# The large mamba stage of a hybrid model: layer-norm turn, channels and step sizes in one block, and the causal convolution as four lagged matrix products

## The reference, cut to what matters

```python
D_MODEL = 128; D_INNER = 256; D_STATE = 16; D_CONV = 4; DT_RANK = 64
residual = x
h = _layernorm(x, ln_g, ln_b)
x_and_res = h @ W_in.T                       # 512 channels
x_h, res = jnp.split(x_and_res, [D_INNER], axis=-1)
xc = jnp.swapaxes(x_h, 1, 2)
xc = lax.conv_general_dilated(xc, conv_w, window_strides=(1,), padding=[(D_CONV - 1, 0)],
                              dimension_numbers=('NCH', 'OIH', 'NCH'), feature_group_count=D_INNER)
x_h = jax.nn.silu(jnp.swapaxes(xc + conv_b[None, :, None], 1, 2))
x_dbl = x_h @ W_x.T
dt, Bm, Cm = jnp.split(x_dbl, [DT_RANK, DT_RANK + D_STATE], axis=-1)
dt = jax.nn.softplus(dt @ W_dt.T + b_dt)
y = _selective_scan(x_h, dt, Bm, Cm, A) + x_h * D_param
y = y * jax.nn.silu(res)
out = y @ W_out.T
return residual + alpha * out
```

## Time and profile before

| | us |
|---|---|
| median of 3 runs | 3471.79 |
| the runs | 3464.45 to 3476.44 |
| the profiled execution | 3465.48 |
| its span in the trace | 3463.7 |

### The profile page before, as it was taken

How to read it: one execution, slowest core, us unless ns; L and a number is a source line. 1 busy time by engine, 2 the same in 40 slices (tenths; PEclk the granted TensorE clock), 3 DMA queues, 4 the chain that set the end, 5 groups by cost and what they waited for, 6 DMA issues and landing times. The chain is left out here.

```text
span 3463.7 us, 62367 instructions
## 1 busy us (share of the span) xinstructions
PE 2799.8 (81%) x21875; PEld 1638.3 (47%) x21951; DVE 2446.1 (71%) x4011; ACT 1755.5 (51%) x3569; POOL 1872.4 (54%) x1198
## 2 busy tenths in 40 slices
PE   3677478568999984999999994677677599999997
PEld 1211266443344431777577751223222277757774
DVE  5599746558777762777577755798699677767764
ACT  3544124134565653777377732543444277637762
POOL 3499211131222212988198812797299598729871
PEclk9699678779999996999999996899799899999999
DMA  3365000033232211122112200343154121212121
GB/s 90 79 164 152 8 1 6 8 114 70 44 51 42 49 22 34 37 44 43 27 41 43 44 21 6 122 158 110 46 167 158 45 44 41 45 25 44 41 45 40
DMA packets 177166, 205.29 MB, mean 59 GB/s; under 512 B 108854, under 2 KB 122893, under 8 KB 176397
## 3 DMA queue, kind: packets, MB, share of 16 engines
q1 hardware_dynamic: 176876, 201.51, 22.9%
HBM read 138.36 MB, written 9.44 MB: 43 GB/s over the span
## 5 line engine op out<-in xcount | busy, mean ns | idle before, releaser
L319 POOL TENSOR_TENSOR arena<-arena 128x1024 f32<-128x1024 f32 x192 | 451.3, 2351 | 61.2 <-DVE arena L336 34.3
L1462 DVE TENSOR_REDUCE causal_peak_parts<-psum 128x1 f32<-128x512 f32 (+3 forms) x608 | 374.9, 657 | 123.0 <-PE psum L1320 79.6
L2060 POOL TENSOR_TENSOR arena<-arena,w_minus_half 128x16 f32<-128x16 f32 x128 | 372.7, 2912 | 95.0 <-DVE arena L1967 95.0
L1429 ACT ACTIVATE arena<-psum 128x512 f32<-128x512 f32 (+1 forms) x608 | 301.4, 596 | 212.1 <-PE psum L1342 92.3
L1902 ACT ACTIVATE arena<-psum,arena 128x128 f32<-128x128 f32 x1024 | 278.7, 384 | 252.2 <-DVE arena L1976 252.2
L336 DVE TENSOR_TENSOR_SCAN arena<-psum,arena 128x1024 f32<-128x1024 f32 x160 | 364.4, 2279 | 28.0 <-POOL arena L319 28.0
L289 ACT ACTIVATE psum<-arena,w_A 128x1024 f32<-128x1024 f32 x192 | 214.4, 1118 | 248.6 <-DVE arena L336 211.4
L2067 POOL TENSOR_TENSOR arena<-arena 128x1024 f32<-128x1024 f32 x124 | 292.6, 2360 | 13.1 <-DVE arena L1961 13.1
L1747 PE MATMUL psum<-w_layer_wqkv,arena 128*128 128x512 f32 x512 | 262.0, 636 | 5.6 <-DVE arena L1961 3.7
L262 PE MATMUL psum<-arena,m_sel 96*128 96x512 bf16 x384 | 117.4, 388 | 180.3 <-DVE arena L351 152.8
L1972 DVE COPY arena<-psum 128x512 f32<-128x512 f32 x128 | 88.5, 691 | 236.6 <-PE psum L1759 236.6
(11 more groups left out here) (331 smaller groups left out, 6565.7 us busy)
## 6 DMA issues: line engine op xcount, KB each, us to landing
arena<-scan_rows_large SPq DMA_DIRECT2D x128, 512.0 KB, 3.7
arena<-arena SPq DMA_DIRECT2D x256, 130.0 KB, 2.6
arena<-scan_rows_small SPq DMA_DIRECT2D x128, 256.0 KB, 3.9
arena<-causal_parts SPq DMA_DIRECT2D x288, 64.0 KB
causal_parts<-arena SPq DMA_DIRECT2D x8, 768.0 KB, 8.3
arena<-Z SPq DMA_DIRECT2D x192, 32.0 KB, 1.9
arena<-Z SPq DMA_DIRECT2D x32, 128.0 KB
arena<-in_c_pads SPq DMA_DIRECT2D x4, 896.0 KB
```

The lines of the kernel that those rows point to most:

```text
L319: pool.tensor_tensor(inputs[:, s % 2], b_lane[:, s % U], du(*runs[o]), ALU.mult).then_inc(input_up.sem, 1)
L1429: act.activation(PT[:, kt % 2, heads[0]:heads[0] + len(heads), lo:hi], place, ACT.Exp, scale=SCALE).then_inc(probs.sem, 1)
L1462: dve.tensor_reduce(part[:, heads[0]:heads[0] + len(heads), qt, half:half + 1].rearrange("p h a -> p (h a)"), place[:, 0:len(heads) * size ...
L2060: pool.tensor_tensor(RN[:, s4, :], SS[:, s4, :], k.minus_half[:, 0:2 * HEADS], ALU.pow).then_inc(rn_in.sem, 1)
```

## The change

`channels` and `deltas` become one function, `prepare`, with one block for each pair. In the first pair this block also holds the turn. The block with the transfer of the selection matrix is gone; its transfer, and one of the rows of `W_in` for the left half (`natural`, 2 x 64 KB), are issued by SyncE in the layer norm's block.

The convolution on VectorE is gone, and so is the copy to LEFT. ScalarE scales the rows of `W_in` by each of the four taps (8 tiles of 128 x 128, in `SC`), TensorE transposes them, ScalarE copies them to `WT`. A left product is then four products that accumulate in the same PSUM banks, each with another tile of WT and with FT read 0, 1, 2 or 3 positions earlier. ScalarE applies silu straight to PSUM.

The products of a sequence stand in one list, `order`: left, left, right, right, t, d, d, b, c. Item n uses two PSUM banks, number n mod 4 of four such pairs, and waits (`free`) until item n - 4 has been read. VectorE waits for the additions of GpSimd one sequence at a time. The copy of B and two copies of C's parts (32 x 1024, to 16 bits) move from ScalarE to VectorE.

```diff
 def mamba_large(k):
...
-    layernorm(k, second_eps=1e-5)
...
+    def load_first(sp):
+        for hf in range(HV):
+            sp.dma_start(natural[:, hf, :], k.dram["L1_attn_b_W_in"][hf * P:(hf + 1) * P, :]).then_inc(loaded.sem, 16)
+        sp.dma_start(selt[:, :], k.dram["c_sel7"]).then_inc(loaded.sem, 16)
+
+    layernorm(k, second_eps=1e-5, sp_first=load_first)
...
-        with nc.Block() as block:
-            @block.sync
-            def _(sp):
-                sp.dma_start(selt[:, :], k.dram["c_sel7"]).then_inc(loaded.sem, 16)
-                sp.wait_ge(loaded.sem, loaded.at(16))
-        for pair in range(BATCH // PAIR):
-            channels(k, pair, two, FT, LEFT, U, R, TMP, HV, KC, PAIR)
-            deltas(k, two, U, DELTA, DU, TMP, REST, PARTS, HV, PAIR, RANK, GAP, NPART, NS,
-                   kept[pair * PAIR:(pair + 1) * PAIR], stored)
...
+    for pair in range(BATCH // PAIR):
+        prepare(k, pair, FT, WT, U, R, DELTA, DU, TMP, REST, PARTS, HV, PAIR, RANK, GAP, NPART, NS,
+                kept[pair * PAIR:(pair + 1) * PAIR], stored, (natural, SC), loaded)
...
+    order = []
+    if pair == 0:
+        order += [("turn", 0), ("taps", 0)] + [("turn", b) for b in range(1, BATCH)]
+    for b in range(PAIR):
+        order += [("left", 2 * b), ("left", 2 * b + 1), ("right", 2 * b), ("right", 2 * b + 1), ("t", b), ("d", 2 * b), ("d", 2 * b + 1),
+                  ("b", b), ("c", b)]
+
+    def two(item):
+        s = order.index(item) % 4
+        return psum[:, 2 * s * BANK:(2 * s + 2) * BANK]
...
+            def turn_taps(place):
+                pe.wait_ge(scaled.sem, scaled.at(1))
+                for n in range(HV * KC):
+                    mm = pe.transpose(place[:, P * n:P * (n + 1)], SC[:, n, :], k.ident)
+                mm.then_inc(taps_up.sem, 1)
+
+            def left(n, place):
+                b, hf = n // HV, n % HV
+                if pair == 0:
+                    pe.wait_ge(normed.sem, normed.at(b + 1))
+                    pe.wait_ge(taps_in.sem, taps_in.at(1))
+                for c in range(2):
+                    for lag in range(KC):
+                        skip = 0 if c else lag
+                        at = (pair * PAIR + b) * SEQ + c * BANK + skip - lag
+                        mm = pe.matmul(place[:, c * BANK + skip:(c + 1) * BANK], WT[:, hf * KC + KC - 1 - lag, :], FT[:, at:at + BANK - skip],
+                                       start=lag == 0, stop=lag == KC - 1, skip_group_check=True)
+                mm.then_inc(left_up.sem, 1)
...
+            for n, item in enumerate(order):
+                if n >= 4:
+                    free(order[n - 4])
...
         @block.scalar
         def _(act):
...
+            if pair == 0:
+                act.wait_ge(loaded.sem, loaded.at(48))
+                for n in range(HV * KC):
+                    sc = act.activation(SC[:, n, :], natural[:, n // KC, :], ACT.Copy, scale=w["conv7_w"][:, n // KC, n % KC:n % KC + 1])
+                sc.then_inc(scaled.sem, 1)
+                act.wait_ge(taps_up.sem, taps_up.at(1))
+                act.activation(WT.rearrange("p n c -> p (n c)"), two(("taps", 0)), ACT.Copy).then_inc(taps_in.sem, 1)
...
+                    act.activation(U[:, hf, b, :], two(("left", n)), ACT.Silu, bias=w["conv7_b"][:, hf:hf + 1]).then_inc(u_up.sem, 1)
...
+            def norm(b):
+                dve.wait_ge(turned.sem, turned.at(b + 1))
+                dve.wait_ge(resid.sem, resid.at(b + 1))
...
+                dve.wait_ge(rest.sem, rest.at(b + 1))
+                dve.tensor_copy(PARTS[GAP:2 * GAP, b, :], REST[GAP:2 * GAP, b, :])
+                dve.tensor_copy(PARTS[2 * GAP:NPART, b, :], REST[2 * GAP:NPART, b, :]).then_inc(mid.sem, 1)
```

More of the change, by code:

```diff
@@ new lines, in mamba_large, with prepare @@
+    mem.close()
+def prepare(k, pair, FT, WT, U, R, DELTA, DU, TMP, REST, PARTS, HV, PAIR, RANK, GAP, NPART, NS, kept, stored, taps, loaded):
+    nc, w, bank, psum = k.nc, k.w, k.bank, k.psum
+    KC = 4
+    names = ("resid", "turned", "normed", "scaled", "taps_up", "taps_in", "left_up", "u", "right_up", "right", "t_up", "dt", "d_up",
+             "size", "decay", "log", "d_taken", "delta", "b_up", "b_taken", "c_up", "first", "rest", "mid", "parts")
+    (resid, turned, normed, scaled, taps_up, taps_in, left_up, u_up, right_up, right, t_up, dt_in, d_up,
+     size, decay, log, d_taken, delta_up, b_up, b_taken, c_up, first, rest, mid, done) = [k.count("m7_" + n) for n in names]
@@ L723, in part_b, with gates, of_channels @@
+            def gates(n, place):
+                b, q = n // HV, HV + n % HV
+                for c in range(2):
+                    at = (pair * PAIR + b) * SEQ + c * BANK
+                    mm = pe.matmul(place[:, c * BANK:(c + 1) * BANK], w["w7_inT"][:, q * P:(q + 1) * P], FT[:, at:at + BANK], start=True, stop=True)
+                mm.then_inc(right_up.sem, 1)
+            def of_channels(b, place, rows, weight, up):
+                pe.wait_ge(u_up.sem, u_up.at(HV * (b + 1)))
                 for c in range(2):
@@ new lines, in _ @@
+                for hf in range(HV):
+                    n = HV * b + hf
+                    act.wait_ge(right_up.sem, right_up.at(n + 1))
+                    act.activation(R[:, hf, b, :], two(("right", n)), ACT.Silu).then_inc(right.sem, 1)
+                for hf in range(HV):
+                    n = HV * b + hf
+                    act.wait_ge(d_up.sem, d_up.at(n + 1))
+                    act.activation(TMP[:, hf, b, :], two(("d", n)), ACT.Abs, bias=w["b7_dt"][:, hf:hf + 1]).then_inc(size.sem, 1)
@@ L829, in _ @@
                     pool.tensor_tensor(DU[:, hf, b, :], DELTA[:, hf, b, :], U[:, hf, b, :], ALU.mult)
-    for s in (t_up, dt_in, b_up, c_up, b_taken, first, rest, mid, done):
+    if pair == 0:
+        for s in (resid, turned, normed):
+            s.passed(BATCH)
+        for s in (scaled, taps_up, taps_in):
+            s.passed(1)
+    for s in (t_up, dt_in, b_up, b_taken, c_up, first, rest, mid, done):
         s.passed(PAIR)
-    for s in (d_up, d_taken, delta_up, size, decay, log):
+    for s in (left_up, u_up, right_up, right, d_up, size, decay, log, d_taken, delta_up):
         s.passed(HV * PAIR)
```

264 lines of the change are left out of this document (102 added, 162 removed).

## The result

| | us |
|---|---|
| before, median of 20 runs | 3469.82 (3459.37 to 3476.44) |
| after, median of 20 runs | 3480.22 (3470.45 to 3486.93) |
| ratio after to before | 1.0034, 95% interval 1.0027 to 1.0042 |
| span of the profiled execution after | 3478.5 |

The change costs 0.34%, some 11.8 us (9.4 to 14.6 by the interval); the two medians lie 10.4 us apart. The forecast was 3475.6 us with a range of 3467 to 3486, and no change within 0.3%. The time lies in the range, but by the ratio just past the 0.3%.

A forecast was written before the change was run, and what follows sets the result against it. No engine was full, since blocks take turns and each preparation's chain counts in full; TensorE's longer list becomes the chain. Second pair +7.0 and first pair -3.2 make +3.8 us on the 3471.79 median: 3475.6 us, range 3467 to 3486.

The forecast's parts named there:

- The sum of the list: TensorE's products in a preparation, waits behind t included: 32.9 us per sequence, 65.8 us per pair.
- rival 2: Left products reading FT shifted, lags 1 to 3, take a quarter longer: +10.3 us, 3485.9 us; chance 6%.
- A cast: In the tail, VectorE's 32-bit to 16-bit copy of a part of C: 0.75 us, upper bound 1.22.
- the tail: From the last C product through copy, subtraction, casts and addition to GpSimd's end: 11.7 us.
- Rival 3: TensorE's list is not the chain and its extra work is hidden: 3461.6 us, faster by 0.29%; chance 5%.
- The first left product: In the first pair, TensorE's start on the left products after turn and transposes: at 2114.5, bounds 2113.7 and 2117.5.
- The eight scalings: In the first pair's lead-in, ScalarE's scalings at 0.388 us each: 3.1 us, until 2108.6.
- the 24 later transposes: First pair, TensorE's transposes besides eight of taps: 0.208 us each, second 16 of all 32 at half cost from 2112.
- My lower bound of 2113.7: Earliest first left product in the first pair, if the clock rises at 2112.
- Rival 1: The clock falls to half speed for 5 us behind each wait behind t: +10 us, 3485.6 us; chance 5%.
- the four waits: TensorE's idle time behind t, before d, while VectorE copies t: 1.28 us each.
- the sum's own upper bound of 8.6: Top of the summed change over both preparations, +2.4 to +8.6 us, with bounds of casts and first left product.

The follow-up runs named there:

- the kernel with the lead-in alone: Kernel before, with only the selection matrix loaded in the layer norm's block and VectorE waiting for one addition at a time: 3464.97 us, ratio 0.9988.
- the run with B behind t: Changed kernel with B's product moved back between t and d, and VectorE's copy of B moved up with it: 3468.33 us, ratio 0.9996.
- one experiment here: Order with B behind t, plus four extra VectorE copies that hold the second left half of each sequence: 3493.71 us, ratio 1.0064.

## Why the prediction was off, by its own steps

**The sum of the list was right.** A record of a left product took 13.88 / 32 = 0.434 us, forecast 0.429, also in lags 1 to 3; rival 2, slow shifted reads, is false. The list of a pair without a fall takes 66.1 us (twice 33.0, from 2424.01 to 2457.02), forecast 65.8. t to d took 5.05 us, forecast 4.9, with 1.40 us idle and not 1.28. A cast takes 0.68 us, forecast 0.75, and the tail 11.6, forecast 11.7. Rival 3 is false: VectorE lost 17 us of work in the second stretch (forecast 18) and nothing came of it. One reading was off without effect: the second d, B and C, which stand between the first d and the item that reuses its banks, are 9.0 us and not 10.8, since the 3.63 us of d are those of both halves. TensorE waited for none of these hand-overs.

**The first left product was mis-sized, by 2.0 us to the good.** It came 7.0 us after the block's start, not 9.0. The eight scalings took 2.45 us, not 3.1. And the 24 later transposes took 2.92 us, 0.12 each: the clock was up 4.5 us after the start and not 6.5 as I had allowed. That is in part the luck of this trace: in the others those 24 took up to 3.87 us, and the first left product came 7.0 to 7.9 us after the start. My lower bound of 2113.7 was 8.2 us after the start, so it was too high as well.

**Rival 1 came true in part, and it is the step that failed.** The sum put nothing on the four waits but their own length. I gave it 5% on the ground that the local transformer idles for pieces of a microsecond at a clock of 1.00. Those gaps are five times shorter in sum over 20 us than one wait here, so the row could not exclude it, as I wrote, and the chance should have followed that. Its form differed: half of the waits are followed by a fall and not all four, but each costs 3.3 us and not 2.5, since the clock is down for some 6.8 us. Together 6.6 us against the 10 that I priced for all four. The Trainium skill, "TensorE: Matmul & The Clock Gate", section "HAM oscillation — how this bites in real kernels", lays repeated throttling to TensorE's idle gaps. These traces agree that without the gap the falls are gone (0 of 8), and differ in that the gap alone doesn't settle it: 0 of 8 between full products.

That the time still lies in the range owes something to luck. The two stretches took 8.75 us more, just past the sum's own upper bound of 8.6. The range holds the time because its upper end had room for the scatter and for mild forms of rival 1, and because the first left product came sooner than forecast.

Put together: forecast +3.8, less 2.0 for the first product, plus 6.6 for the falls, plus 0.3 for waits and list, is +8.7, and the two stretches show +8.75. The ratio says 11.8, with 9.4 at its lower end (the medians say 10.4). The rest lies in stages whose instructions are the same. They scatter: the turn begins at 2105.48 before, and with identical code ahead of it at 2107.56, 2099.71 and 2117.04 in traces shown above. Whether a microsecond or two of the measured loss is real there, the runs don't settle.

**Where the expected gain went.** The change shortens the lead-in by 11.5 us, from 18.6 to 7.0 us after the turn's start (7.5 of them come in the kernel with the lead-in alone), and spends them and more: 24 records more per sequence on TensorE, whose list of 66 us then is the chain, while VectorE, relieved of 17 us, waits. The run with the convolution back on VectorE shows what the rest is worth without this trade: 38 us against the kernel before, of which some 7 are the lead-in. How the rest divides between the single block and the second sequence's place in the new order wasn't parted. Against the run with B behind t, which has one block for each pair as well, its two preparations are 126.1 us and not 158.6.

**What stays open.** What lets the clock fall behind a short gap. Shown: filling the wait ends it, a longer wait at this place brought it in 4 of 4 cases (one trace), and gaps of the same length between the left halves did not bring it in 8 cases. Were all 28 gaps alike and independent, 0 of 8 against 11 of 20 would be luck in about 1 of 100 cases; but the waits behind t don't look independent, so this is a rough figure. And a gap of 3.28 us ahead of t, in the kernel with the convolution on VectorE, passed without a fall. Whether it is the narrow products (t 64 columns, B 16, d 64 rows) or something else about that place wasn't parted.

## What to carry to other kernels

When work moves from an engine that isn't the bound to another, write down the receiving engine's whole list first: it may become the chain, as here, although no engine was full. Keep TensorE's list without holes: a product that is independent belongs between a producer and the product that waits for the copy of it, and the hole can cost more than its length: here four holes of 1.40 us cost 5.6 us by themselves and 6.6 more by the two falls behind them. And read where the time went, not only how much: one experiment here hit the number of a theory that its trace disproved.

## What the runs showed of the hardware

- Behind a short gap the clock fell while TensorE was at work again: in the six falls behind waits of 1.40 us it stayed at 1.00 for 1.3 to 2.6 us after the wait, then was at 0.50 for some 6.8 us, with TensorE busy. In pauses of 5.0, 6.8 and 8.0 us it fell within the pause, 2.1 to 4.8 us after the pause had begun. Two falls, one behind a wait of 2.63 us and one in a pause of 6.8 us, lasted 10.2 us.
- The same gap, the same code and the same place gave both outcomes from one execution to the next (6 of 12, one in each preparation).
- TensorE with 8 products more was 6.6 us faster by median than without (3473.64 and 3480.22 us, in two sets of runs; the ratios to the kernel before are 1.0015 and 1.0034), and by the traces 4.0 us (165.0 and 169.0 for both preparations).
- A copy from 32 to 16 bits on VectorE, 32x1024 inside SBUF, took 0.68 us. A transfer of 2 KB inside SBUF held TensorE for 1.8 us from the last product to the next.
